# One unit's TensorE work regrouped: scores with the projection, the four mixes together, four buffers for the exponentials

## What is computed

```
qkv = (h @ Wqkv.T).reshape(b, n, 3, H, HD)
q = _ln(qkv[:, :, 0].transpose(0, 2, 1, 3), qn_g, qn_b)
k = _ln(qkv[:, :, 1].transpose(0, 2, 1, 3), kn_g, kn_b)
v = qkv[:, :, 2].transpose(0, 2, 1, 3)
scores = jnp.einsum('bhnd,bhmd->bhnm', q, k) / jnp.sqrt(jnp.float32(HD))
attn = jax.nn.softmax(scores, axis=-1)
o = jnp.einsum('bhnm,bhmd->bhnd', attn, v)
o = o.transpose(0, 2, 1, 3).reshape(b, n, H * HD)
x = x + o @ Wout.T
```

## Time and profile before

| | |
|---|---|
| time, median of 3 runs | 422.96 us (422.95 to 424.42) |
| profiled execution | 422.88 us, span 421.1 us |
| PE busy | 399.4 us (95%) |
| ACT, DVE, POOL busy | 284.7, 275.9, 193.7 us |
| chain that ended last | PE 81%, DVE 10%, POOL 4% |
| granted PE clock | 0.998 of full |

### The profile page before, as it was taken

One profiled execution on the slowest core, in us unless ns is written; L12 is line 12 of the kernel. 1 busy time (PEld: TensorE's weight loads), 2 busy tenths in 40 slices (PEclk: granted clock), 3 DMA queues, 4 the chain that ended last, 5 costly groups with the idle time before them and its releaser, 6 DMA issues.

```text
span 421.1 us, 8341 instructions
## 1 busy us (share of the span) xinstructions
PE 399.4 (95%) x2738; PEld 341.5 (81%) x2738; DVE 275.9 (66%) x648; ACT 284.7 (68%) x532; POOL 193.7 (46%) x203
## 2 busy tenths in 40 slices
PE   6999997899999999999999999999999997789996
PEld 5578666778899889989988998899898786566894
DVE  3666556776666676677676666766775736987733
ACT  3357566677788777778777887777777337759441
POOL 7500416485657756775776577567757000300000
PEclk9999999999999999999999999999999999999999
DMA  5760000191000000000000000000000000000001
GB/s 133 212 133 1 2 2 0 38 362 52 0 3 2 0 2 1 2 2 0 2 2 0 0 0 1 0 0 0 1 0 2 0 2 1 2 2 0 2 2 50
DMA packets 7792, 10.67 MB, mean 25 GB/s; under 512 B 403, under 2 KB 4302, under 8 KB 7758
## 3 DMA queue, kind: packets, MB, share of 16 engines
q1 hardware_dynamic: 6718, 9.73, 8.0%
q10 hardware_dynamic: 1040, 0.52, 0.4%
HBM read 8.68 MB, written 0.52 MB: 22 GB/s over the span
## 4 chain that ended last, share of the span: by engine, by line
PE 81%; DVE 10%; POOL 4%; issue 3%; ACT 2%; DVEq 0%; POOLq 0%; ACTq 0%
PE pair L1489 27%; PE pair L1440 10%; PE pair L1460 7%; PE bank L1479 6%; PE bank L1474 6%; PE pair L1245 4%; PE pair L1715 2%; PE pair L1727 2%; PE pair L1329 1%; PE pair L1405 1%; PE pair L1617 1%; PE bank L1245 1%; POOL rstd L455 1%; PE pair L1672 1%; PE pair L1354 1%
## 5 line engine op out<-in xcount | busy, mean ns | idle before, releaser
L1489 PE MATMUL pair<-v_s,probs_T 128*128 128x129 f32 x1024 | 128.4, 275 | 0.6 <-ACT probs_T L702 0.6
L1489 PEld LDWEIGHTS pair<-v_s,probs_T 128*128 128x128 f32 x1024 | 124.5, 191 | 4.6 <-ACT probs_T L702 0.9
L1016 DVE TENSOR_REDUCE negmax<-pair 128x1 f32<-128x512 f32 x128 | 88.5, 691 | 55.1 <-PE pair L1460 54.8
L702 ACT ACTIVATE probs_T<-bank 128x512 f32<-128x512 f32 x128 | 73.1, 597 | 48.7 <-PE bank L1479 39.4
L500 POOL TENSOR_TENSOR q_s<-kq,k_s 64x512 fp32r<-64x512 f32 x29 | 37.2, 1282 | 73.5 <-DVE k_s L1004 73.5
L1460 PE MATMUL pair<-k_s,q_s 128*128 128x512 f32 x128 | 56.4, 441 | 0.7 <-DVE negmax L1016 0.7
L490 POOL TENSOR_TENSOR qk_rstd<-qk_ms,minus_half 128x8 f32<-128x8 f32 x32 | 53.2, 1661 | 2.6 <-POOL qk_ms L486 0.2
L1474 PE MATMUL bank<-q_s,k_s 128*128 128x512 f32 x128 | 51.1, 399 | 0.0
L1479 PE MATMUL bank<-q_shift,k_low 128*128 128x512 f32 x128 | 50.7, 396 | 0.2 <-DVE q_shift L1023 0.2
L1038 DVE SCALAR_TENSOR_TENSOR x_att<-pair,o_rec,x_att 128x128 f32<-128x128 f32 x128 | 38.6, 344 | 1.1
L500 POOL TENSOR_TENSOR k_low<-kq,k_s 64x512 fp32r<-64x512 f32 x29 | 36.7, 1265 | 2.2
(11 more groups left out here) (292 smaller groups left out, 697.5 us busy)
## 6 DMA issues: line engine op xcount, KB each, us to landing
fc_raw<-in_L_cond_fc2s_dram SPq DMA_DIRECT2D x1, 2048.0 KB, 13.8
x_in<-in_x_dram ACTq DMA_DIRECT2D x1, 512.0 KB, 3.9
w<-in_L_cond_mlp_w_dram SPq DMA_DIRECT2D x2, 256.0 KB, 2.9
wout<-in_L_cond_Wout_dram SPq DMA_DIRECT2D x1, 512.0 KB
k_low<-k_low SPq DMA_DIRECT2D x1, 512.0 KB, 8.0
q_shift<-q_shift SPq DMA_DIRECT2D x1, 512.0 KB, 9.4
b_all<-in_L_cond_b2s_dram SPq DMA_DIRECT2D x1, 512.0 KB, 10.9
out_dram<-final SPq DMA_DIRECT2D x2, 256.0 KB, 2.2
```

The source lines that it names most:

```text
L702: act.activation(probs_T[:, k % 2, :], bank[2 + k % 2][:, :], ACT.Exp).then_inc(exp_done, 1)
L1016: dve.tensor_reduce(negmax[:, c:c + 1], bank[0][:, :], AX, ALU.max, negate=True).then_inc(max_done, 1)
L1489: last = pe.matmul(pair4[:, c // 2, c % 2 * (D + 1):(c % 2 + 1) * (D + 1)], probs_T[:, k % 2, c * P:c * P + P], v_s[:, r % (2 * PAIRS), k, :],
```

## The change

On PE, time u is put into another order. Before: S0, ST0, ST1, half a projection, S1, the other half, ST2, S2, T, M0, M1, S3, ST3, M2, shifts, M3. After: S0, ST0, ST1, S1, half a projection, ST2, S2, the other half, ST3, S3, T, M0, M1, M2, shifts, M3. On DVE each row maximum from the second on moves ahead of one half of `unit_out` or of the piece work. On ACT the exponentials of k = 2 and k = 3 each move ahead. Two more buffers for exponentials (`probs_far`) lie in memory that is not in use at that time. No instruction is added or taken away.

```diff
+        probs_far = Area(early.at + 4 * N)("probs_far", [P, 2, N])
...
+        def probs(k, at=slice(0, N)):
+
+            return (probs_T, probs_far)[k // 2][:, k % 2, at]
...
             def keys_exp(u, k):
                 wait(act, st_done, 4 * u + k + 1)
-                wait(act, pv_done, 4 * u + k - 1)
-                act.activation(probs_T[:, k % 2, :], bank[2 + k % 2][:, :], ACT.Exp).then_inc(exp_done, 1)
+                wait(act, pv_done, 4 * u + k - 3)
+                act.activation(probs(k), bank[2 + k % 2][:, :], ACT.Exp).then_inc(exp_done, 1)
...
                     q_high_beside(u + 1, r + 1)
+                if back:
+                    keys_exp(u - 1, 2)
                 if arriving:
                     piece_square(u + 3)
                     piece_copy(u + 3, r + 3)
                 if turning:
                     piece_affine(u + 2)
                 if back:
-                    keys_exp(u - 1, 2)
+                    keys_exp(u - 1, 3)
                 if turning:
                     q_high(u + 2, r + 2)
-                if back:
-                    keys_exp(u - 1, 3)
-                if turning:
                     k_high_beside(u + 2, r + 2)
...
                 if live:
                     row_max(u, 0)
+                    row_max(u, 1)
                 if leaving:
                     unit_out(u - 2, r - 2, 0)
                 if live:
-                    row_max(u, 1)
+                    row_max(u, 2)
                 if leaving:
                     unit_out(u - 2, r - 2, 1)
                 if live:
-                    row_max(u, 2)
+                    row_max(u, 3)
                 if due(u, 0, UNITS - 4):
                     piece_ss(u + 3)
                 if turning:
                     piece_high(u + 2, r + 2)
                 if live:
-                    row_max(u, 3)
                     shift_row(u, r)
...
-                                     probs_T[:, k % 2, c * P:c * P + P], v_s[:, r % (2 * PAIRS), k, :],
+                                     probs(k, slice(c * P, c * P + P)), v_s[:, r % (2 * PAIRS), k, :],
...
-                if due(u, 0, UNITS - 4):
-                    project(u + 3, r + 3, head, (0,))
                 if live:
                     scores(u, r, 1)
                 if due(u, 0, UNITS - 4):
-                    project(u + 3, r + 3, head, (1,))
+                    project(u + 3, r + 3, head, (0,))
                 if back:
                     scores_T(u - 1, r - 1, 2)
                 if live:
                     scores(u, r, 2)
+                if due(u, 0, UNITS - 4):
+                    project(u + 3, r + 3, head, (1,))
+                if back:
+                    scores_T(u - 1, r - 1, 3)
+                if live:
+                    scores(u, r, 3)
...
                 if back:
-                    mix(u - 1, r - 1, 0)
-                    mix(u - 1, r - 1, 1)
-                if live:
-                    scores(u, r, 3)
-                if back:
-                    scores_T(u - 1, r - 1, 3)
-                    mix(u - 1, r - 1, 2)
+                    for k in range(NC - 1):
+                        mix(u - 1, r - 1, k)
                 if live:
                     shifts(u, r)
                 if back:
-                    mix(u - 1, r - 1, 3)
+                    mix(u - 1, r - 1, NC - 1)
```

## The result

The changed kernel takes 430.0 us (median of 4 runs, 428.9 to 431.05) against 422.95 before: a ratio of 1.0152, with an interval of 1.0118 to 1.0186. Its profiled execution took 428.90 us with a span of 427.1, so +6.02 against the profiled one of before.

What follows compares the result with a forecast made beforehand. PE was taken as the bound, busy for all 223.80 us of times 2 to 28. Terms 3.8 + 1.3 + 1.7 - 0.4 - 0.2 = +6.2 on 422.9 gave 429.0 us, range 425.5 to 432.5 (about 0.8).

Steps and rivals of the forecast that it cites:

- S1 behind ST1, times 2 to 28: On PE, S1 waits 0.14 us for the first row maximum in each of 27 times: +3.8 us (2.7 to 4.6).
- S0 ahead of even times: S0 waits for the copied keys of T's piece in 13 even times, 4 to 28: +1.3 us (0 to 2.0).
- times 29 to 31: Without projection, S1, S2 and S3 each wait for the maximum before: +1.7 us (1.4 to 2.0).
- time 32: ST3 moves into the gap before the logits' weight load: -0.4 us (0 to -0.5).
- ahead of time 2: An exponential's 0.66 us wait for a mix goes, but copies behind it wait for DVE: -0.2 us (0 to -0.66).
- S2 and S3: In the loop, the second and third maxima end in time with 0.09 us to spare each; nothing added.
- What would show it: Signs: PE no longer fills times 2 to 28, PEld idles 0.3 us each time, S0 starts about 8.43 us apart.
- Later maxima that are late: Rival: S2 and S3 in the loop also wait; a tenth beyond cover for both gives 434.4 us; chance 0.12.
- No wait in the loop: Rival: S1 and even S0 get data in time, only the last times count: 424.0 us; chance 0.06.
- A price for the change between kinds of matmul: Rival: two changes instead of four on PE save time; at 0.15 us each, 420.9 us; chance 0.04.
- The clock: Rival: small waits drop PE from 2.4 to 1.2 GHz for a tenth of the loop: 451 us; chance 0.02.
- A faster run of 512 columns: Rival: the run of 18 512-column matmuls on PE has shorter steps, 0.22 us each: 425.2 us; chance 0.04.

Runs made afterwards that it cites:

- the two kernels that fell short here: Changed kernel with one projection matmul ahead of S1, one ahead of S2, T ahead of S3: 433.91 us; changed kernel with only T ahead of S3: 435.69 us.

## Why the prediction was right, step by step

Sign, time (429.0, by its terms 429.1, against 430.0 and 428.90 profiled) and the main cause held. The terms, in us, against the profiled executions:

| term | forecast | measured |
|---|---|---|
| S1 behind ST1, times 2 to 28 | +3.8 | +3.33 |
| S0 ahead of even times | +1.3 | +0.87 |
| projection behind S1, loop's turn | none | +0.90 |
| times 29 to 31 | +1.7 | +1.55 |
| time 32 | -0.4 | -0.51 |
| ahead of time 2 | -0.2 | -0.21 |
| rest | | +0.09 |

*S1.* The wait read at the earlier trace rows stood in the loop too, 0.123 each and not 0.14. The runs with S1 one step earlier and with half a maximum move it by what the matmuls and the maximum's length say, in both directions.

*S2 and S3.* No wait shows at either in times 2 to 28, so the 0.09 to spare was enough. In times 29 to 31 the pattern came as reckoned; 7.80 and 7.81 instead of 7.86.

*S0 of even times.* The size was about right, but it hung on less than was said. Thirteen times were counted and eleven waited, 6 to 26. Written out, the chain from T to S0 just fits (4.04 between the rows of T and S0 in every time, without a wait). In the loop the copy ends 3.96 after T, against 3.88 written out, since T to affine takes 0.72 there and 0.64 here. That alone makes no wait: time 28, the first behind the loop, also has 3.96, and its S0 loads its weights 0.05 after the copy and doesn't wait. In the loop they load 0.13 after it. So the wait lies in these two hand-overs together; POOL's opening, from which the working took its upper end, was 0.08 as at the lower one.

*Not forecast.* The turn of the loop and the projection behind S1 made 0.90 together, which is what S1 and S0 fell short by (0.47 + 0.43). That much of the agreement in the sum is chance.

*What would show it.* One sign was wrong: PE does fill the window (229.08 of 229.10). A wait of 0.12 lies under the row of the matmul ahead, as the first timeline above shows. The step that failed is the one from a late start to idle time. The row of S1 in the earlier trace rows carries no idle time either; times 30 and 31 did show 0.23 of idle in the earlier trace rows, but each had longer holes as well. The other signs came: PEld's 0.3 in each of 27 times, and starts of 8.41 and a little more ahead of even times.

*The rivals.* Later maxima that are late: no wait at S2 or S3. No wait in the loop: there is one in every time. A price for the change between kinds of matmul: the loop written out has two changes in each time instead of four, and without S1's wait it takes 223.84 against 223.81, so there is no gain of that kind. The clock: 1.00 in the windows of times 2 to 32, with a small wait in every time, so the drop that the Trainium skill describes (TensorE: Matmul & The Clock Gate, "A second HAM failure mode: psum-queue depth-cycling") was not seen here. A faster run of 512 columns: the steps after the change, behind S2, were

```profile
267.64 0.39 PE L1464 MATMUL pair<-k_s,q_s 128*128 128x512 f32 x1
...
269.26 0.60 PE L1249 MATMUL pair<-ident,qk_n 128*128 128x128 f32 x4
```

Seven steps in 1.62, or 0.231 each, as in the earlier trace rows. The section that the prediction names there of the Trainium skill (TensorE: Matmul & The Clock Gate, "Back-to-back issue gap") gives the 216 ns for a matmul by itself and about 131 ns for a stream of them. The 231 ns here, in a stream, agrees with neither.

## What to carry to other kernels

Work that stands between a producer and the step that must wait for its consumer is cover, even where it looks like an interruption of a run; count its length against the whole round trip (here 1.28 from S0 to S1, of which the maximum itself is 0.69) before it is moved. A step moved on one engine moves the place of its consumers in the other engines' lists, which are worked in order: the two kernels that fell short here did so on DVE, and one exchange of two instructions there gave back 7.5 us of the loop (232.03 to 224.51). The gain was to be had where PE was idle already, in the last times, and not in the loop where its list had no gap.

## What was not expected of the hardware

- A matmul of 512 columns has a row of 0.40 us at steps of 0.231. So a short wait leaves PE's busy column full, and only PEld's idle time and the distance of the starts show it: 27 waits of 0.123 here, 3.33 us at 229.08 busy of 229.10. Of a wait of 0.59 the column showed 0.32.
- Behind the loop's branch ACT's first exponential opens late, 1.45 after S0 before and 1.94 after the change, where the loop's other times mostly have 1.05 to 1.08. It costs only where the slack is gone (0.28 here).
- In the loop some hand-overs are 0.08 us longer than written out (T to affine 0.72 against 0.64; S0 to the first exponential 1.07 against 0.98; ACT's copy to S0's weight load 0.13 against 0.05 at time 28).
